# Fp32 graph layers split into high and low parts: aligned buffers, a first chunk in halves, one sum sooner, the scale on GpSimd and a last block in three steps

## What is computed

```python
xw = x @ weight
scale = jnp.sum(d_list * filt * d_list, axis=0)
out = adj @ (scale[:, None] * (adj @ xw)) + bias
x = layernorm(x + out)
deg = lambda A: jnp.sum(A, axis=1, keepdims=True)
X_in = (adj / deg(adj)) @ x @ W_in
X_out = (adj.T / deg(adj.T)) @ x @ W_out
x = layernorm(x + X_in + X_out)
```

## Time and profile before

| | us |
|---|---|
| median of 3 runs | 754.64 (754.17 to 755.7) |
| profiled execution | 754.41 |
| its span | 752.6 |
| PE busy | 740.1 |
| DVE busy | 552.9 |
| ACT busy | 475.0 |
| GpSimd busy | 0.2 |

### The profile page before, as it was taken

One profiled execution on the slowest core, in us unless ns is written; L12 is line 12 of the kernel. 1 busy time (PEld: TensorE's weight loads), 2 busy tenths in 40 slices (PEclk: granted clock), 3 DMA queues, 4 the chain that ended last, 5 costly groups with the idle time before them and its releaser, 6 DMA issues. The chain is left out here.

```text
span 752.6 us, 9059 instructions
## 1 busy us (share of the span) xinstructions
PE 740.1 (98%) x3337; PEld 605.5 (80%) x3337; DVE 552.9 (73%) x673; ACT 475.0 (63%) x1167; POOL 0.2 (0%) x4
## 2 busy tenths in 40 slices
PE   8999999999999999999999999999999999999995
PEld 5878888888888888788888888888887888888884
DVE  4896865838373464787665647988679999899994
ACT  5996673837263543234343446998799888877771
POOL 0000000000000000000000000000000000000000
PEclk9999999999999999999999999999999999999999
DMA  9998875656656445255455459999989999999981
GB/s 325 411 375 342 356 264 214 258 215 209 216 191 223 168 168 224 78 209 207 178 175 217 167 197 373 381 385 381 382 303 371 384 366 373 381 358 336 348 350 29
DMA packets 35532, 208.64 MB, mean 277 GB/s; under 512 B 3616, under 2 KB 8480, under 8 KB 11040
## 3 DMA queue, kind: packets, MB, share of 16 engines
q1 hardware_dynamic: 35072, 207.86, 73.5%
q10 hardware_dynamic: 416, 0.20, 0.1%
HBM read 205.95 MB, written 2.10 MB: 276 GB/s over the span
## 5 line engine op out<-in xcount | busy, mean ns | idle before, releaser
L376 DVE TENSOR_TENSOR lo<-raw,hi 128x2048 fp32r<-128x2048 f32 x184 | 417.0, 2287 | 139.4 <-ACT hi L274 104.6
L274 ACT ACTIVATE hi<-raw 128x512 fp32r<-128x512 f32 x512 | 315.5, 620 | 60.8 <-DMA raw<-in_adjT_b 38.4
L575 PE MATMUL accA<-hi,x_hi 128*128 128x512 f32 x512 | 203.1, 397 | 1.4 <-ACT x_hi L282 0.7
L578 PE MATMUL accA<-hi,x_lo 128*128 128x512 f32 x512 | 200.3, 391 | 0.3 <-DVE x_lo L381 0.3
L277 ACT ACTIVATE hi<-raw 128x2048 fp32r<-128x2048 f32 x64 | 121.7, 1912 | 72.1 <-DMA raw<-in_adjT_b 72.1
L584 PE MATMUL accA<-lo,x_hi 128*128 128x512 f32 x512 | 138.5, 392 | 0.8 <-DVE lo L376 0.8
L575 PEld LDWEIGHTS accA<-hi,x_hi 128*128 128x128 f32 x512 | 96.2, 188 | 23.1 <-ACT hi L274 2.0
L584 PEld LDWEIGHTS accA<-lo,x_hi 128*128 128x128 f32 x512 | 95.9, 188 | 22.8 <-DVE lo L376 1.7
L578 PEld LDWEIGHTS accA<-hi,x_lo 128*128 128x128 f32 x512 | 96.2, 188 | 20.8 <-DVE x_lo L381 0.6
L575 PE MATMUL accB<-hi,v_hi 128*128 128x512 f32 x256 | 101.2, 395 | 0.9 <-DVE turned L433 0.9
L578 PE MATMUL accB<-hi,v_lo 128*128 128x512 f32 x256 | 100.1, 391 | 0.0
(11 more groups left out here) (66 smaller groups left out, 461.4 us busy)
## 6 DMA issues: line engine op xcount, KB each, us to landing
raw<-in_adjT_b SPq DMA_DIRECT2D x127, 1024.0 KB, 4.9
raw<-in_adj_b SPq DMA_DIRECT2D x64, 1024.0 KB, 5.0
rows<-in_xT_b SPq DMA_DIRECT2D x8, 256.0 KB, 9.8
rows<-in_x_t SPq DMA_DIRECT2D x8, 256.0 KB, 5.9
out<-rows SPq DMA_DIRECT2D x7, 256.0 KB, 5.6
raw<-in_adjT_b SPq DMA_DIRECT2D x4, 256.0 KB, 5.0
out<-rows SPq DMA_DIRECT2D x1, 128.0 KB, 1.9
out<-rows ACTq DMA_DIRECT2D x1, 128.0 KB, 1.9
```

The costliest lines, as they stand in the source:

```text
L274: nc.scalar.activation(hi[slot][:, t], raw[slot][:, t], ACT.Copy, accum_out=sums[:, TPB * K + t, C:C + 1]).then_inc(s_hi, 1)
L376: nc.vector.tensor_tensor(lo[slot][:], raw[slot][:], hi[slot][:], ALU.subtract).then_inc(s_lo, 1)
L575: nc.tensor.matmul(acc, r_hi[:, TPB * K + t], h[:, t], start=(first and t == 0), stop=False)
L578: nc.tensor.matmul(acc, r_lo[:, TPB * K + t], h[:, t], start=False, stop=False)
```

## The change

- The ring is rounded down to a multiple of 2048 bytes (slot 0 at byte 129024), and an unused piece in front of x_hi brings it to 18432, so x_hi, x_lo, v_hi, v_lo, rows, part and turned start at multiples of 2048.
- Chunk 0 comes in two halves: tiles 0 and 1 on SP's queue, tiles 2 and 3 on ACT's, behind W0. ACT makes x_hi behind tile 0 instead of behind tile 1.
- The scale's four instructions go to GpSimd, which waits for the small loads; `v_block(0)` waits for their semaphore.
- `turn_z(7)` on ACT and `v_block(7)` on DVE stand one chunk earlier; `o_sum(6)` stands ahead of `x1_parts(7)`.
- The last block: copy in 1 + 3 tiles, products and updates in 1 + 1 + 2 tiles.
- `h_block` and `update` lose the wait for DVE's own count ahead of them; behind `update` it is kept only ahead of the statistics.

```diff
-        ring_at = nc.sbuf_top // 64 * 64 - 2 * RING * CHUNK
+        ring_at = nc.sbuf_top // LINE * LINE - 2 * RING * CHUNK
...
+        pair_at = -(-nc.sbuf_base // LINE) * LINE
+        sb("unused", [P, (pair_at - nc.sbuf_base) // 32 * 8])
         x_hi = sb("x_hi", [P, NT, P], F32R)
...
-            for t in range(TPB):
-                sp.dma_start(raw[0][:, t], adjT_b[J, I, :, t]).then_inc(s_piece[t], 16)
+            sp.dma_start(raw[0][:, 0:2], adjT_b[J, I, :, 0:2]).then_inc(s_piece[0], 16)
...
             act.dma_start(w0[:], W0).then_inc(s_w0, 16)
+            act.dma_start(raw[0][:, 2:4], adjT_b[J, I, :, 2:4]).then_inc(s_piece[1], 16)
...
-                    split(0, range(0, 2))
+                    split(0, range(0, 1))
                     x_parts(0)
-                    split(0, range(2, TPB))
+                    split(0, range(1, TPB))
...
-                if n == N1 + 1:
+                if n == N1:
                     turn_z(NB - 1)
...
-            for at in (slice(0, 2 * P), slice(2 * P, 4 * P)):
+            for at in (slice(0, P), slice(P, 4 * P)):
                 nc.scalar.activation(turned[:, 1, at], accA[:, 1, at], ACT.Copy).then_inc(s_lh, 1)
...
+        @block.gpsimd
+        def _(pool):
+            pool.wait_ge(s_small, 16 * len(small))
+            nc.gpsimd.tensor_tensor(ctmp[:], coef[:, 0], coef[:, 1], ALU.mult).then_inc(s_pool, 1)
+            pool.wait_ge(s_pool, 1)
+            nc.gpsimd.tensor_tensor(ctmp[:], ctmp[:], coef[:, 0], ALU.mult).then_inc(s_pool, 1)
+            pool.wait_ge(s_pool, 2)
+            for k in range(1, KD):
+                to = s_sc if k == KD - 1 else s_pool
+                first = ctmp[:, 0] if k == 1 else scale[:]
+                nc.gpsimd.tensor_tensor(scale[:], first, ctmp[:, k], ALU.add).then_inc(to, 1)
...
             def v_block(I):
+                if I == 0:
+                    dve.wait_ge(s_sc, 1)
...
             def update(k, r, tiles, e):
                 dve.wait_ge(s_n, e + 1)
-                dve.wait_ge(s_nat, e - NB)
-                if k >= NB + 2:
-                    dve.wait_ge(s_out, k - NB - 1)
...
-                dve.wait_ge(s_nat, e - NB + 1)
...
                 if n == N1 + 3:
                     x1_block(NB - 1)
+                    o_sum(NB - 2)
                     x1_parts(NB - 1)
-                    o_sum(NB - 2)
...
-            update(k, r, range(0, 2), NAT_Y[r])
-            update(k, r, range(2, 4), NAT_Y[r] + 1)
+            dve.wait_ge(s_out, k - NB - 1)
+            update(k, r, range(0, 1), NAT_Y[r])
+            update(k, r, range(1, 2), NAT_Y[r] + 1)
+            update(k, r, range(2, 4), NAT_Y[r] + 2)
+            dve.wait_ge(s_nat, NAT_Y[r] + 3 - NB)
...
-            by_rows(NAT_Y[r], NAT_Y[r], w_in, range(0, 2))
+            by_rows(NAT_Y[r], NAT_Y[r], w_in, range(0, 1))
             pe.wait_ge(s_lh, 2)
-            by_rows(NAT_Y[r] + 1, NAT_Y[r], w_in, range(2, 4))
+            by_rows(NAT_Y[r] + 1, NAT_Y[r], w_in, range(1, 2))
+            by_rows(NAT_Y[r] + 2, NAT_Y[r], w_in, range(2, 4))
```

More of the change, by code:

```diff
@@ L17 @@
 EPS = 1e-5
+LINE = 4 * BLK
 WARM = 9
@@ L177, in graph_kernel @@
         s_small = sem("small_loaded")
-        s_piece = [sem(f"first_chunk_loaded{t}") for t in range(TPB)]
+        s_piece = [sem(f"first_chunk_half_loaded{h}") for h in range(2)]
         s_raw = [sem(f"raw_loaded{r}") for r in range(RING)]
@@ L184, in graph_kernel @@
         s_hi = sem("hi_ready")
+        s_pool = sem("pool_step")
+        s_sc = sem("scale_ready")
         s_tz = sem("turned_by_act")
@@ L272, in split @@
                         if n == 0:
[L273 removed]
+                            act.wait_ge(s_piece[t // 2], 16)
                         nc.scalar.activation(hi[slot][:, t], raw[slot][:, t], ACT.Copy,
@@ L356, in _ @@
             store(nc.scalar, NB - 1, range(2, 4))
+        @block.gpsimd
[9 more added lines that the diff above has]
+                nc.gpsimd.tensor_tensor(scale[:], first, ctmp[:, k], ALU.add).then_inc(to, 1)
+                if k < KD - 1:
+                    pool.wait_ge(s_pool, k + 2)
         @block.vector
@@ L391, in inverse @@
                 then(nc.vector.reciprocal(deg[:, k, at], a))
-            def scales():
-                dve.wait_ge(s_small, 16 * len(small))
-                then(nc.vector.tensor_tensor(ctmp[:], coef[:, 0], coef[:, 1], ALU.mult))
-                then(nc.vector.tensor_tensor(ctmp[:], ctmp[:], coef[:, 0], ALU.mult))
-                then(nc.vector.tensor_tensor(scale[:], ctmp[:, 0], ctmp[:, 1], ALU.add))
-                for k in range(2, KD):
-                    then(nc.vector.tensor_tensor(scale[:], scale[:], ctmp[:, k], ALU.add))
             def biased(b):
@@ L495, in update @@
                 last.then_inc(s_nat, 1)
-                dve.wait_ge(s_nat, e - NB + 1)
             def out_block(k, r):
+                if k >= NB + 2:
+                    dve.wait_ge(s_out, k - NB - 1)
                 update(k, r, range(TPB), NAT_Y[r])
+                dve.wait_ge(s_nat, NAT_Y[r] + 1 - NB)
                 moments(k, r, range(TPB))
```

6 lines of the change are left out of this document (2 added, 4 removed).

## The result

| | before | after |
|---|---|---|
| median | 754.64 us (753.93 to 755.7, 5 runs) | 747.19 us (745.93 to 747.96, 5 runs) |
| ratio | 1 | 0.9899, 95% interval 0.9884 to 0.9913 |
| profiled execution | 754.41 us | 747.96 us |
| its span | 752.6 us | 746.2 us |

The kernel became 7.45 us faster. I had forecast 752.0 us, 2.55 us of gain by the sum of the terms, and a range of 750.1 to 753.6: the sign was right, the size was not, and the time lies outside the range.

What follows compares the result with a forecast made beforehand. TensorE, busy 740.1 of 752.6 us, bounds the kernel. Start 0.8, scale 0.1, sum 1.2 and tail 0.45 make 2.55 us, taking the profiled 754.41 to 751.86 and the median to 752.1; stated 752.0, range 750.1 to 753.6.

Steps and rivals of the forecast that it cites:

- Moved buffers: Rows of raw, hi and lo no longer cross a 2048-byte line: 0 us, bounds 49 us gained or as much lost.
- Rival (4): Buffers all at multiples of 2048 make reads meet, each matmul starts later: 758.1 us at 2 ns per matmul; chance 0.07.
- Rival (5): Crossing the 2048-byte line does cost matmuls: 742.8 us at 3 ns per matmul; chance 0.08.
- The sooner sum: Near 305 us DVE's addition moves ahead of block 7's normalisation, so PE's wait and slow first matmul go: 1.2 us.
- Tail: Last block: shorter first copy, fewer matmul instructions and waits between updates: 0.45 us gained, from 0 to 0.65.
- Scale on GpSimd: DVE loses four small instructions; PE's wait for lo of chunk 9 goes, one for v_lo comes: net 0.1 us, 0 to 0.5.
- Rival (3): GpSimd blocks DVE or is late, PE waits for lo at 38 to 43 us: 752.5 to 753.0 us; chance 0.07.
- Start: Chunk 0 in halves on two queues raises the load rate before 8 us, chunk 1 starts sooner: 0.8 us, bounds 0 and 1.6.
- So the later half is just hidden: Start: despite the first tile's later half, PE is ready for chunk 1 at 12.7 us, before chunk 1 at 12.9.
- (1): The start gains nothing, since the slow load rate before 8 us is the chip's cold start: 752.8 us; chance 0.17.
- (2): The start loses: the first half lands as late as the third quarter did, 0.75 us lost: 753.55 us; chance 0.08.

Runs made afterwards that it cites:

- both sides 64 short: The changed kernel with the ring and x_hi both 64 bytes short of a multiple of 2048, so that tiles cross lines again: 748.48 us.
- the moves alone: The kernel before with the ring and x_hi both moved to multiples of 2048 bytes and nothing else of the change: 748.19 us, ratio 0.9917.
- the front undone: The changed kernel with chunk 0 again in four quarters on SP's queue and x_hi behind tile 1: 747.03 us, in a later chip run 746.74.
- third job: One chip run with the kernel before (754.80 us), the changed kernel (747.35), the front undone (746.74), and halves on SP's queue with lo of chunk 8 in tiles (745.72).
- second job: One chip run: kernel before 754.21 us, changed kernel 745.66, and it with eight unused matmuls 745.87, quarters on two queues 745.91, halves on SP's queue 745.66.
- mixed kernel: The changed kernel with slot r of the ring moved by 32 x r bytes and v_hi and v_lo by 160 bytes: 760.33 us.

## Why the prediction was wrong, point by point

**Moved buffers: 0 us forecast, 6.0 to 6.4 measured. This is the step that failed** ("A crossing costs nothing there. I take 0"). The two bounds, 49 us either way, were wide enough. What went wrong is the row that decided between them. The spacing was the first sign of being wrong that I had named ("A spacing other than 229 would break the forecast at once"), and it is the one that came. The earlier trace rows compare a buffer that crosses a line with one that doesn't, and there I was right: crossing costs nothing, the kernel with both sides 64 short shows it. But the edit changed a second property too, how the moving tile lies to the weights, 64 bytes off modulo 256 before and 0 after. No row of the trace of before could price this, because all of its large matmuls have the same distance. The rows did hold a warning that I wrote down and dropped: 512 columns at 2.4 GHz are 213 ns, and the starts stand 229 apart. A gap of 16 ns on each of 3072 matmuls, with no cause known, is 49 us of ignorance; zero with a narrow range around it wasn't what it supports.

**The rivals on this step.** Rival (4) said that equal alignment makes reads collide and the kernel slower. Equal alignment is the cheapest case of all. The price that it feared, 2 ns a matmul and more, does exist: 3.7 and 4.2 ns, if only one side moves. Rival (5) had the sign and nearly the size (3 ns forecast, 2.1 measured), and gave the line as the cause; its 742.8 and my 752.0 lie on either side of the 747.19. Its cause is refuted: that it comes near the measured time is luck. A chance of 0.08 for any gain of this kind was too small.

**The sooner sum: 1.2 us forecast, 1.14 measured.** In the kernel with the moves alone the wait is still there (product 102 to 103 takes 3.87 us), with the sum moved it is 2.72, which is a product without a wait. The rows of the moves alone show it as the earlier trace rows did:

```profile
302.57 0.50 PE L578 MATMUL accB<-hi,v_hi 128*128 128x512 f32 x1 [0.98 <-DVE turned L436]
```

**Tail: 0.45 us forecast, 0.3 measured.** From the copy's start to that of the statistics it is 2.99 us before and 2.74 after, and the stretch behind product 255 is 0.3 shorter than with the moves alone (11.76 and 11.46). Each step came as worked out, and each a little longer: the first update 0.94 us behind the copy's start (0.88 forecast), the third step at 1.34 (1.24), its result 0.76 later (0.66).

**Scale on GpSimd: 0.1 us forecast; too small to measure here.** Product 12 stands 36.79 us behind chunk 1's first matmul with the front undone and 36.90 with the moves alone, which still has the scale on DVE; but a second execution with the front undone has 37.23, so this difference of 0.1 shows nothing. The waits came as forecast. The wait for lo of chunk 9 went, as forecast, and v_lo became late instead: the start behind it is at 51.76, where 51.43 would follow from 50.52 and four matmuls. GpSimd took 2.6 us for four instructions (0.79, 0.72, 0.58, 0.25) that DVE did in 0.95, with 13 us to spare. This price, unknown in the forecast, was hidden as said: PE waits for none of it. Rival (3) is nearly empty: two of DVE's tiles that ran beside it took 1.67 us together,

```profile
32.65 1.67 DVE L392 TENSOR_TENSOR lo<-raw,hi 128x512 fp32r<-128x512 f32 x2
```

where two of the same kind without it took 1.30:

```profile
28.41 1.30 DVE L392 TENSOR_TENSOR lo<-raw,hi 128x512 fp32r<-128x512 f32 x2
```

The 0.37 us are far from any wait of PE. The Trainium skill's rule of the shared port (page "SBUF — State Buffer", the section named above) has one of the two wait for the whole instruction of the other. The trace shows less than that: DVE's tiles were stretched by a quarter and not held for the 0.6 to 0.8 us of one GpSimd instruction.

**Start: 0.8 us forecast; nothing measured in the median.** Of its chain of steps most held. The rate rose to 360 GB/s and then to 428 (340 forecast in the middle). The first tile was ready at 6.37 to 7.21 us (6.4 forecast), and in the execution in which the clock stayed up chunk 1's first matmul came at 12.78 (12.9 forecast). What I had left out is PE's clock: the later half leaves PE idle for 1.99 us in the profile, where it had been 0.69, and behind it the clock fell to the 1.2 GHz level. Chunk 1 came at 15.20, 2.42 us behind the other execution: 0.84 of that lie ahead of product 0 (the half landed at 7.21 instead of 6.37), 1.58 behind its first matmul. The sign that I had named for this term, a first matmul of chunk 1 later than 13.7, is there in two of the changed kernel's three profiled executions. In the third job the kernel with the front undone is 0.6 us faster than the changed one, whose profiled execution there had the low clock. Where the clock stays up, the new start does gain: by the ratios to the kernel before (0.9887 in the second job, against 0.9894 and 0.9902 with the front undone) I estimate 0.5 to 1.1 us, from different chips. So the loads' part of the term was about right, and what failed is the step "So the later half is just hidden": it took PE's longer wait to cost nothing but its own length. Rivals (1) and (2) are nearer to the measured median than the forecast: (1)'s nothing is the right size for another reason (the rate does rise), and (2) has the sign of the executions in which the clock falls.

**The sum, with the measured terms:** 6.2 (moves) + 1.15 (sum) + 0.3 (tail) + 0.1 (scale, as forecast) - 0.3 (start) = 7.45. The last term isn't measured: it is what is left between the others and the medians, and with 6.0 to 6.4 for the moves it is -0.1 to -0.5. Without the moves the forecast of 2.55 would by this reckoning have been too high by 1.3 us, nearly all of it the start.

## What to carry to other kernels

- Where an edit moves buffers, ask what it does to the place of each pair of operands that one instruction reads, not only to each buffer by itself. For fp32r matmuls of 512 columns with 128 x 128 weights, the one form tried here, keep the weights' and the moving tile's start a multiple of 256 bytes apart: it is worth up to 7 ns of 233, and 17 to 18 us of 748 in this kernel.
- A spacing above what the columns need is an open question with a size. Until an experiment with shifted buffers has closed it, the range has to hold it.
- A start that leaves PE idle just before its first long chain can cost more in the clock than it gains in the loads. Compare starts where the waits behind them are over (here at product 12), over several profiled executions.

## What the runs showed of the hardware that I had not expected

- The spacing of fp32r matmuls (512 moving columns, 128 x 128 weights) by the distance modulo 256 bytes: 226.7 to 227.1 ns at 0, 229.1 at 64, 232.8 at 128, 233.3 at 192, when all matmuls have the same; 232 to 235 at 32, 96, 160 and 224 in the mixed kernel. Even 226.7 is 13 ns more than 512 columns at 2.4 GHz, and where these come from stays open.
- The spacing depends on what came before: in the mixed kernel the first five matmuls of a product at distance 0, behind a product at another distance, stand 232 ns apart (729.37 to 730.53 us), and in the changed kernel so do those behind four transposes (233 ns, 298.02 to 299.42 us).
- Behind 2.03 us of idling PE kept its full clock, behind 1.4 us it fell to 1.2 GHz, in two executions of the same kernel.
- Two DVE instructions beside GpSimd's took 0.37 us longer together, and GpSimd needed 2.6 us for what DVE did in 0.95.
